# Self and cross attention: maxima products in pairs of PSUM banks, scores and exponentials one head at a time

## The reference

```
h1 = _ln(x, n1_g, n1_b)
x = _attn(h1, h1, q1, k1, v1, o1_w, o1_b, heads) + x          # self: 512 queries, 512 keys
h2 = _ln(x, n2_g, n2_b)
x = _attn(h2, context, q2, k2, v2, o2_w, o2_b, heads) + x     # cross: 512 queries, 1024 keys
...
sim = jnp.einsum('bhid,bhjd->bhij', q, k) * scale
a = jax.nn.softmax(sim, axis=-1)
out = jnp.einsum('bhij,bhjd->bhid', a, v)
```

## Time and profile before

| | us |
|---|---|
| median of 3 runs (884.85 to 887.86) | 886.52 |
| the profiled execution | 892.92 |
| its span, first to last instruction | 891.1 |
| TensorE / VectorE / ScalarE / GpSimd busy | 818.8 / 602.6 / 473.5 / 101.6 |
| items, TensorE (L917), both stages and the first layer | 227.9 |
| scores, TensorE (L954) | 204.0 |
| reductions of 512 columns (L1084), maxp and negm | 251.0 + 121.3 |
| exponentials (L1048) | 311.6 |

### The profile page before, as it was taken

The page is one execution under the profiler, slowest core; times in us unless marked ns, Lnnn a source line. Parts: engine busy times, 40 slices in busy tenths (PEclk is TensorE's granted clock), DMA queues, the critical chain, the costliest instruction groups (busy, mean ns, idle before and its releaser), DMA issues.

```text
span 891.1 us, 11402 instructions
## 1 busy us (share of the span) xinstructions
PE 818.8 (92%) x4148; PEld 450.8 (51%) x4148; DVE 602.6 (68%) x1111; ACT 473.5 (53%) x708; POOL 101.6 (11%) x142
## 2 busy tenths in 40 slices
PE   5899999999989988899999759999999999899998
PEld 4776544444566655333334523333333333578888
DVE  4555567776772545599975597999999981865241
ACT  4633444545552521576677506767667778574130
POOL 4100005000022331000002500000000000220000
PEclk9999999999997999599999957999999999999999
DMA  8887587424210163212208410222233000600000
GB/s 297 273 276 207 134 261 228 115 65 119 63 46 23 68 214 105 72 55 64 64 11 133 152 38 1 55 54 55 54 55 55 1 2 1 252 0 1 30 1 30
DMA packets 30966, 83.18 MB, mean 93 GB/s; under 512 B 5172, under 2 KB 9212, under 8 KB 28606
## 3 DMA queue, kind: packets, MB, share of 16 engines
q1 hardware_dynamic: 30110, 79.71, 31.5%
q0 software_dynamic: 800, 2.73, 0.9%
HBM read 56.12 MB, written 25.89 MB: 92 GB/s over the span
## 4 chain that ended last, share of the span: by engine, by line
PE 60%; DVE 22%; DMA 8%; issue 4%; ACT 4%; SPq 2%; POOL 0%; ACTq 0%; DVEq 0%; POOLq 0%
PE PS L974 17%; PE PS L917 12%; PE PS L1538 8%; DVE maxp L1084 8%; PE PS L954 6%; PE PS L618 5%; DVE negm L1084 5%; DMA k_d<-split 5%; PE PS L1556 4%; PE PS L1340 3%; DVE maxp L1098 2%; DMA q_sl<-msplit 2%; DVE turned L1130 2%; ACT probs L1048 1%; DMA w_v<-in_Wv 1%
## 5 line engine op out<-in xcount | busy, mean ns | idle before, releaser
L1048 ACT ACTIVATE probs<-PS 128x1024 f32<-128x1024 f32 (+1 forms) x336 | 311.6, 971 | 145.1 <-PE PS L954 141.2
L1084 DVE TENSOR_REDUCE maxp<-PS 128x1 f32<-128x512 f32 (+1 forms) x400 | 251.0, 679 | 42.2 <-PE PS L917 41.2
L917 PE MATMUL PS<-k_sl,q_sl 48*128 48x512 f32 (+2 forms) x592 | 227.9, 456 | 15.9 <-DVE negm L1084 5.4
L954 PE MATMUL PS<-q_sl,k_sl 50*128 50x512 f32 (+3 forms) x672 | 204.0, 435 | 9.6 <-ACT probs L1048 4.7
L917 PEld LDWEIGHTS PS<-k_sl,q_sl 48*128 48x128 f32 (+2 forms) x592 | 103.6, 190 | 174.7 <-DVE maxp L1084 105.7
L1084 DVE TENSOR_REDUCE negm<-PS 128x1 f32<-128x512 f32 (+1 forms) x192 | 121.3, 679 | 29.3 <-PE PS L917 29.2
L954 PEld LDWEIGHTS PS<-q_sl,k_sl 50*128 50x128 f32 (+2 forms) x672 | 103.3, 192 | 57.5 <-ACT probs L1048 23.7
L974 PE MATMUL PS<-probs,v2c 128*32 128x512 f32 x640 | 87.5, 616 | 1.0
L660 DVE TENSOR_TENSOR split<-PS,split 128x512 fp32r<-128x512 f32 (+3 forms) x54 | 34.9, 650 | 60.5 <-ACT split L635 60.3
L974 PE MATMUL PS<-probs,v0c 128*64 128x512 f32 (+1 forms) x256 | 62.0, 605 | 0.0
L635 ACT CAST split<-PS 128x512 fp32r<-128x512 f32 (+3 forms) x54 | 29.9, 554 | 56.4 <-PE PS L618 39.8
(11 more groups left out here) (185 smaller groups left out, 1059.6 us busy)
## 6 DMA issues: line engine op xcount, KB each, us to landing
k_d<-split SPq DMA_DIRECT2D x20, 512.0 KB, 3.9
q_d<-split SPq DMA_DIRECT2D x12, 512.0 KB, 4.0
k_sl<-k_d SPq DMA_DIRECT2D x8, 640.0 KB
k_sl<-k_d SPq DMA_DIRECT2D x40, 128.0 KB
q_sl<-q_d SPq DMA_DIRECT2D x40, 128.0 KB
k_sl<-k_d SPq DMA_DIRECT2D x20, 256.0 KB
w_raw<-in_ff_w SPq DMA_DIRECT2D x1, 3840.0 KB, 12.2
k_sl<-k_d SPq DMA_DIRECT2D x8, 320.0 KB
```

Source lines behind the costliest of these rows:

```text
L917: nc.tensor.matmul(PS[0:a.qt, SBANKS[k % 3], 0:cn], q_view(g)[f:f + a.rows, j // a.stack, q * a.qt:(q + 1) * a.qt], k_view(g)[f:f + a.rows ...
L954: mm = nc.tensor.matmul(PS[0:sz, 2 * (x % 2) + half, 0:a.nq], k_view(g)[f:f + a.rows + 2, j // a.stack, t * 128:t * 128 + sz], q_view(g)[f ...
L1048: nc.scalar.activation(probs[0:a.size[t], x % PRING, :, 0:a.nq], PS[0:a.size[t], 2 * (x % 2):2 * (x % 2) + 2, 0:a.nq], ACT.Exp, scale=a.sc ...
L1084: nc.vector.tensor_reduce((maxp if nch > 1 else negm)[0:a.qt, g.turn, o:o + 1], PS[0:a.qt, SBANKS[k % 3], 0:a.chunks[c][1]], AX.X, ALU.max ...
```

## The change

1. Items are made in pairs (`item_pair`), on banks 4, 5 or 6, 7 in turn (`PAIR_BANKS`); one reduction reads both banks (`reduce_pair`). A pair waits for the pair before the last.
2. Scores are made head by head (`score_head`) on banks 0, 1, 2 in turn (`SCORE_BANKS`), and each head has its own exponential of 512 columns. A head waits for the exponential of the head three places before (`slot_freed`). Flips after the lead take a place in this ring; flips in the self lead take one in the ring of pairs.
3. The order on TensorE for step s becomes: heads 0 and 1 of step s+1, first pair, head 2, both value pairs of step s, head 3, second pair, flip.
4. The output bank of both stages becomes 3; the projections `selfp` keep banks 2 and 3 and lose bank 7.
5. In the lead of self attention a pair follows each of the two projections of a chunk, on TensorE and VectorE.
6. The high and low parts of the maxima are made on GpSimd (`pool_maxima`), between its scalings. In cross attention VectorE still joins the two chunks' maxima.

The first layer's attention keeps its order. The diff, cut (the semaphore counts, `sp_load` waits and choice of the bank of a flip follow from it):

```diff
+SCORE_BANKS = (0, 1, 2)
+PAIR_BANKS = (4, 6)
...
+    def place_pairs(self):
+
+        self.pair_use, self.pair_freed, pairs = {}, [], 0
+        self.head_slot, self.flip_slot, self.slot_freed = {}, {}, []
+        for c in range(len(self.steps)):
+            ended, items = self.chunk(c)
+            for i, m in items[::2]:
+                pairs += 1
+                self.pair_use[i, m] = len(self.pair_freed)
+                self.pair_freed.append(("items", 2 * pairs))
+            if ended is not None and c < self.lead:
+                self.flip_use[ended] = len(self.pair_freed)
+                self.pair_freed.append(("flip", ended + 1))
+        for s in range(len(self.steps)):
+            for h in range(4):
+                self.head_slot[s, h] = len(self.slot_freed)
+                self.slot_freed.append(("exp", 4 * s + h + 1))
+            for c in self.chunks_at(s - 1) if s > 0 else []:
+                ended, _ = self.chunk(c)
+                if ended is not None:
+                    self.flip_slot[ended] = len(self.slot_freed)
+                    self.slot_freed.append(("flip", ended + 1))
...
-    selfp = Projection("selfp", self_jobs(), (2, 3, OBANK))
+    selfp = Projection("selfp", self_jobs(), (2, 3))
+        st.obank = 3 if st.stacked else OBANK
...
+        def pair_free(k):
+            if k >= 2:
+                by, n = st.pair_freed[k - 2]
+                pe.wait_ge(st.score_free if by == "items" else st.flipped, n)
+
+        def slot_free(k):
+            if k >= 3:
+                by, n = st.slot_freed[k - 3]
+                pe.wait_ge(st.exp if by == "exp" else st.flipped, n)
+
+        def item_pair(i, m):
+            g = st.groups[i]
+            a = g.a
+            k = st.pair_use[i, m]
+            if m == 0:
+                pe.wait_ge(q_loaded[g.place], g.loads)
+            pair_free(k)
...
+        def score_head(s, h):
+            i, t = st.steps[s]
+            g = st.groups[i]
+            a = g.a
+            sz = a.size[t]
+            k = st.head_slot[s, h]
+            if t == 0 and h == 0:
+                pe.wait_ge(g.m_sem, g.m_loads)
+            slot_free(k)
...
-            pe.wait_ge(st.exp, x + 3)
+            pe.wait_ge(st.exp, 2 * x + 2 if st.stacked else x + 3)
...
+            elif side is self_side:
+                pairs = st.chunk(x)[1][::2]
+                for ph, j in side.share(x):
+                    pe_projection(pe, ph, [j])
+                    for i, m in pairs[:1]:
+                        item_pair(i, m)
+                    pairs = pairs[1:]
+                for i, m in pairs:
+                    item_pair(i, m)
+                flips([x])
...
+            for h in range(4):
+                score_head(0, h)
             for s in range(len(st.steps)):
-                if s + 1 < len(st.steps):
-                    scores(*st.steps[s + 1], 0)
-                maxima(st.chunks_at(s), 0, 2)
-                if s + 1 < len(st.steps):
-                    scores(*st.steps[s + 1], 1)
-                maxima(st.chunks_at(s), 2, 3)
+                pairs = [p for c in st.chunks_at(s) for p in st.chunk(c)[1][::2]]
+                following = s + 1 < len(st.steps)
+                if following:
+                    score_head(s + 1, 0)
+                    score_head(s + 1, 1)
+                for i, m in pairs[:1]:
+                    item_pair(i, m)
+                if following:
+                    score_head(s + 1, 2)
                 for p in range(2):
                     values(*st.steps[s], p)
-                maxima(st.chunks_at(s), 3)
+                if following:
+                    score_head(s + 1, 3)
+                for i, m in pairs[1:]:
+                    item_pair(i, m)
                 flips(st.chunks_at(s))
...
-            for p in range(a.pairs):
+            for h in range(4 if st.stacked else 0):
+                act.wait_ge(st.used, 2 * s + h // 2 + 1)
+                act.wait_ge(st.pair, 4 * s + h + 1)
+                nc.scalar.activation(probs[0:a.size[t], (2 * s + h // 2) % PRING, h % 2, 0:a.nq],
+                                     PS[0:a.size[t], SCORE_BANKS[st.head_slot[s, h] % 3], 0:a.nq],
+                                     ACT.Exp, scale=a.scale).then_inc(st.exp, 1)
...
+            if nch == 1 and st is not S_FIRST:
+                return
...
+        def reduce_pair(i, m):
+            g = st.groups[i]
+            a = g.a
+            dve.wait_ge(st.score, st.item_at[i, m] + 2)
+            nch = len(a.chunks)
+            to = (maxp if nch > 1 else negm)[0:a.qt, g.turn, 0:a.cols * nch].rearrange("p (e u) -> p u e", e=2)
+            first = PAIR_BANKS[st.pair_use[i, m] % 2]
+            nc.vector.tensor_reduce(to[:, m // 2, :], PS[0:a.qt, first:first + 2, :],
+                                    AX.X, ALU.max, negate=nch == 1).then_inc(st.score_free, 2)
...
+            elif side is self_side:
+                ended, items = st.chunk(x)
+                if ended is not None:
+                    part_maxima(ended)
+                for n, (ph, j) in enumerate(side.share(x)):
+                    for i, m in items[2 * n:2 * n + 2:2]:
+                        reduce_pair(i, m)
+                    dve_projection(dve, ph, [j])
+                for i, m in items[2 * len(side.share(x))::2]:
+                    reduce_pair(i, m)
...
+    def pool_maxima(pool, st, i):
+        g = st.groups[i]
+        a = g.a
+        if len(a.chunks) > 1:
+            pool.wait_ge(st.negated, st.negated_to[i])
+        else:
+            pool.wait_ge(st.score_free, st.item_at[i, len(a.items) - 1] + 1)
+        m = negm[0:a.qt, g.turn, 0:a.cols].rearrange("p (e c) -> p e c", e=a.stack)
+        parts = mparts[0:a.qt, g.turn, 0:2 * a.cols].rearrange("p (e s c) -> p e s c", e=a.stack, s=2)
+        nc.gpsimd.tensor_copy(parts[:, :, 0, :], m).then_inc(st.m_high, 1)
+        pool.wait_ge(st.m_high, i + 1)
+        nc.gpsimd.tensor_tensor(parts[:, :, 1, :], m, parts[:, :, 0, :].bitcast(F32),
+                                ALU.subtract).then_inc(st.m_low, 1)
...
+    def pool_groups(pool, st, first):
+        for i in range(len(st.groups)):
+            pool_scale(pool, st, i)
+            if i + first < len(st.groups):
+                pool_maxima(pool, st, i + first)
```

More of the change, by code:

```diff
@@ L846, in sp_cross @@
         for i in range(SLOTS):
-            sp.wait_ge(before.pair, before.pairs_to(len(before.groups) - SLOTS + i))
+            sp.wait_ge(before.pair, before.scores_to(len(before.groups) - SLOTS + i))
             sp_load_k(sp, st.groups[i])
@@ L900, in wide_items @@
                 flip(st.chunk(c)[0], waits=False)
+        def pair_free(k):
[13 more added lines that the diff above has]
+            pair_free(k)
+            for e in range(2):
+                j, q, c = a.items[m + e]
+                c0, cn = a.chunks[c]
+                f = a.base(j)
+                nc.tensor.matmul(PS[0:a.qt, PAIR_BANKS[k % 2] + e, 0:cn],
+                                 q_view(g)[f:f + a.rows, j // a.stack, q * a.qt:(q + 1) * a.qt],
+                                 k_view(g)[f:f + a.rows, j // a.stack, c0:c0 + cn],
+                                 start=True, stop=True).then_inc(st.score, 1)
+        def score_head(s, h):
[7 more added lines that the diff above has]
+            slot_free(k)
+            f = a.base(h)
+            nc.tensor.matmul(PS[0:sz, SCORE_BANKS[k % 3], 0:a.nq],
+                             k_view(g)[f:f + a.rows + 2, h // a.stack, t * 128:t * 128 + sz],
+                             q_view(g)[f:f + a.rows + 2, h // a.stack, :],
+                             start=True, stop=True).then_inc(st.pair, 1)
         def bank_free(k):
@@ L995, in pe_attention @@
                 pe.wait_ge(ph.padded, ph.nv)
-        one = st.groups[0].a.pairs == 1
-        for s in range(2 if one else 1):
-            for p in range(st.groups[0].a.pairs):
-                scores(*st.steps[s], p)
+        one = not st.stacked
         if one:
+            for s in range(2):
+                scores(*st.steps[s], 0)
             for s in range(0, len(st.steps), 2):
```

84 lines of the change are left out of this document (53 added, 31 removed).

## The result

The changed kernel takes 922.79 us (median of 4 runs, 915.28 to 931.52), the kernel before 887.19 beside it (4 runs, 884.85 to 889.36): ratio 1.037, 95% interval 1.026 to 1.048. The forecast was 891.8, with 885 to 900 as the range. The sign was right, the size was not. The profiled execution took 915.28, its span is 913.3, against 892.92 and 891.1 before.

The account below looks back on a forecast made before the run. The order of work on three maxima banks, not any engine's work, was taken to bound a step (2.70 us). Stretch terms, from -7.9 for the lead to +7.4 for the cross end, made +5.3 on 886.5: 891.8, range 885 to 900.

Parts of the forecast that it names:

- the stall at group ends: At group ends, value products wait for the output bank's turn behind the last wide reduction: 3.67 us, 1.06 over 2.61.
- Its two rivals on the clock: Clock stays up in the first self group, 886.4 us, chance 0.13; clock falls in the tails, 899, chance 0.10.
- the tail rival: Both tails: TensorE's short idleness each step lowers the clock; 20 us at half clock adds 7, 899 us, chance 0.10.
- The ring's link from head 3 to its exponential: In each step's 2.61 us cycle of waits on three score banks: 0.53 us, as from product to reduction.
- The flip: Where a maxima flip takes a place among three score banks: about 0.45 us more, between 0.2 and 0.6.
- GpSimd was to release no flip: Maxima copies moved to GpSimd, 0.3 us each, end before the flip, so GpSimd is never its releaser; cost nothing.
- The lead: Self attention's lead, with pairs between projections: first value products at 355.0 against 362.86, 7.9 us earlier.
- the rival in which the clock stays up: First self group after the lead: shorter waits may avoid half clock, about 12.5 us for 17.9, time 886.4, chance 0.13.
- The tails: Steps without maxima in self and cross attention: 2.61 us instead of about 2.0; self tail +4.8, cross end +7.4.
- VectorE as the bound: Main parts: steps near 2.35 us, 0.26 less over 84 of them, -22, time 870, chance 0.05.
- without a saving from the wide reduction: Wide reduction takes 1.36 us: ordinary steps still 2.61, 0.15 more at 16 group ends, time 894, chance 0.06.
- without a gain in the lead: Self attention's lead: a load or store ends last, 1.8 us per projection caught, time 899, chance 0.06.

Follow-up runs that it names:

- a_turn_first: Changed kernel, with VectorE turning the output bank ahead of the second wide reduction in a group's last step: 891.05 us against 888.62 for the kernel before.
- g: Kernel before, with only the output bank's turn moved behind the first two reductions of the next step in self and cross attention: 933.23 us against 883.92.
- i: Kernel before, with only the output bank's turn moved behind one reduction of the next step: 915.21 us against 888.23.
- f_turn_swap: Changed kernel, with the output bank turned ahead of the second wide reduction and ScalarE's two waits in their old order: 879.99 us against 883.92 for the kernel before.
- b_wait_swap: Changed kernel, with ScalarE's two waits before each exponential put back in the order of the kernel before: 923.46 us, ratio 1.038.
- j: Changed kernel with earlier turn, old wait order, and scores by pair in both tails from one step later: 865.22 us against 888.23 for the kernel before.
- c_heads_only: Kernel before, with only scores and exponentials by head on three banks, old maxima kept: 983.49 us, ratio 1.079.
- e_heads_four: Kernel before, with only scores and exponentials by head, on four score banks, old maxima kept: 919.77 us against 883.92.
- h: Changed kernel with earlier turn, old wait order, and scores and exponentials by pair in both tails: 869.65 us against 883.92 for the kernel before.

## Why the prediction was wrong, step by step

By the landmarks of both profiled executions (first value products, starts of the joins), predicted and measured differences:

| stretch | predicted | measured |
|---|---|---|
| self lead | -7.9 | -6.9 |
| first self group | +0.6 | -1.0 |
| seven self groups (82.53 to 90.73) | +2.2 | +8.2 |
| self tail | +4.8 | +8.6 |
| join and first cross group | 0 | -0.5 |
| seven cross groups (158.54 to 163.21) | -1.8 | +4.7 |
| cross end | +7.4 | +8.6 |
| after it | 0 | +0.5 |
| sum | +5.3 | +22.2 |

- **The step that failed: the sum prices an idle wait at its own length.** The text had the stall at group ends right, place, cause and size (3.67 forecast, 3.73 measured, with 0.2 more where the packed tile's turn precedes, forecast 0.3), and then wrote 1.06 us for it. Its two rivals on the clock looked at the first group and the tails, and none at the main parts. That TensorE was idle for 4.78 of 83.29 us at full clock stands there against the clock falling in the tails; but that idleness comes in pieces of at most 0.13 us all over the stretch, and the new one at group ends in one piece of 1.0 to 1.2. In the profiled execution the stretches that followed cost: 15.59 and 14.66 for groups that else take about 12.1, twice 24.89 for 22.65, one step of 3.82 for 2.67, and in the self tail 12.4 us from 473.80 to the end of the last value products, where the same four steps took 8.6 in a_turn_first at full clock: 3.5 + 2.6 + 4.5 + 1.2 + 3.7 = 15.5 us, 11.8 of them behind the pauses at group ends. The 3.7 of the self tail are not: there the fall comes 2.3 us after a group that starts without a pause, and it belongs to the tail rival. For the main parts a in one direction, g and i in the other show cause and effect. The way from +22.4 between the profiled executions to +35.6 between the medians is the place of each in its runs: 5.7 above the median before, 7.5 below it after, where two other runs had a mean clock of 0.917 and 0.914, not 0.938, and took 13.6 and 16.2 us longer than the profiled one.
  The Trainium skill, "TensorE: Matmul & The Clock Gate", section on psum-queue depth-cycling, was named for the tails. In the tails, where each step has its pause of about 0.5 us, the traces go both ways: a_turn_first, with TensorE busy for 9.17 of 10.59 us in four steps of its cross tail, kept 1.00 there, f_turn_swap and b_wait_swap fell. In the main parts of the changed kernel it was the one long pause, not small ones at each bank.
- **The ring's link from head 3 to its exponential.** 0.53 was taken from a product and its reduction on VectorE, 0.60 was measured, since the change also turns the order of ScalarE's two waits. Both lines stand in the diff, and the text has no part on them. Over some 107 steps it is 6.4 us of the miss, worked out from the steps; b, with the old order, was no faster in the time. With the old order the ring is 2.60 to 2.61 (b, f, j), the number of the text.
- **The flip** costs 0.24 (2.91 for 2.67), not 0.45: over some 15 flips 3 us in the other direction. Together the three come to 19 us of the miss of 16.9; the lead adds 1.0, the first group takes off 1.6, the rest is in smaller terms, the ends of the tails above all.
- **Sizes that held.** Exponential 0.60 (602 ns), wide reduction 1.21 (1219 ns), its second bank free of charge, copies on GpSimd 0.20 and 0.22 us, a bank's turn as releaser at group ends, head 2 released by the exponential. One sign did not hold: GpSimd was to release no flip, and it released one in the wide lead of cross attention, with TensorE idle for 1.92 us before it. Before, VectorE released that flip after 1.70, so it cost 0.2 us.
- **The lead** came out at 355.98 for 355.0 partly by luck. The first product started at 319.34 and not at 320.81, as one projection fewer stands before it, and from there to the value products it took 36.6 us and not 34.2, with the lower clock for 6.8 us from 319.1. (The parts listed add up to 27.8 without the overlaps that the text takes off 28.2, so the total used is right.)
- **The first group** was at 0.67 and not 0.52 mean clock, 16.3 us for 17.9: a piece of the rival in which the clock stays up.
- **The tails** had their 2.66 us a step, and the self tail also 10.2 us at the lower clock: the tail rival (0.10), smaller than its 20 us and beside the forecast, not in its place. It shows in the traces of b, c, e and f too and not in that of a, and what decides is open.
- The rivals with VectorE as the bound, without a saving from the wide reduction and without a gain in the lead are out, by 2.67, 1219 ns and 355.98.

The range failed because every case in it, but for the two clock rivals, moved by the lengths of waits; none had the clock falling in the main parts.

## What to carry to other kernels

A pause of TensorE can cost more than its length: here 1.0 to 1.2 us once in a group brought the clock down behind some of the groups, for 3 to 14 us at a time, and one instruction of 0.7 us moved ahead of a reduction gave back 32 us, about half of it the waits and half the clock. So when instructions on another engine get twice as long, look at what is queued behind them in front of TensorE, and put what frees TensorE's bank first. And when a diff touches the order of two waits, it is an edit with a price (0.06 us a time here).

## What was not expected of the hardware

- How small a pause is enough. With 1.15 us once in four steps (i, self) the clock fell in six of seven groups, with 1.00 once in eight (changed kernel, cross) behind three of eight group ends, with 0.72 once in eight (i, cross) never. But length and distance alone don't decide. With 1.00 to 1.21 once in four (changed kernel, self) it fell behind two of eight, with 1.32 once in eight (g, cross) behind one of eight, and two single pauses brought none: the one of 1.21 us before 462.69 in the kernel before, and h's of 2.23 us before 448.56. What else counts is open.
- ScalarE starts 0.53 us after the product when the wait on the product is tested first, and 0.60 after it when a wait long fulfilled is tested first and this one second.
- The lower clock can last with TensorE at work: 102.4 us in c_heads_only, with TensorE recorded busy for 90.23 of them and, from 552.89 on, for 73.81 of 73.81. Ends of matmuls are modelled, so small pauses may be hidden in that. Why it stayed there, and left after 54.6 us in e_heads_four, is open.
